# Biases of V and of the output projection as one more matmul each, x normalised on GpSimd, the residual added on VectorE, softmax divided in one pass, features later

## What is computed

```python
x = x + jnp.tanh(g_xattn[0]) * _L0_xattn_ref(_layernorm(x, axis=-1), ctx_1024, ctx_1024, ...)
x = x + jnp.tanh(g_ffn[0]) * _L0_ffn_ref(_layernorm(x, axis=-1), L0_ffn_w1, L0_ffn_w2)

# _L0_xattn_ref: 16 heads of width 32
Q, K, V = query @ Wq.T + bq, key @ Wk.T + bk, value @ Wv.T + bv
scores = Q @ K^T / sqrt(32)
feats = [scores.mean, scores.max(-1).mean, var(softmax(scores), ddof=1).mean]   # per head
t = exp(clip(w3 . gelu(w2 . gelu(w1 . feats + b1) + b2) + b3))                   # a temperature per head
out = softmax(Q @ K^T / (2 t)) @ V
return out @ Wo.T + bo

# _L0_ffn_ref: rows of x quantised to 8 bits, weights to -1, 0, 1
h = gelu(_bitlinear(x, w1)); return _bitlinear(h, w2)
```

## Time and profile before

| | |
|---|---|
| device time, median of 3 runs | 1525.43 us (1525.19 to 1525.73) |
| span of the profiled execution | 1523.1 us (the page gives no other time for it) |
| median less that span | 2.3 us |
| busy: PE, DVE, ACT, POOL | 1247.1, 1187.1, 958.2, 429.1 us |
| mean granted clock of TensorE | 0.91 |
| one turn of the loop (end of the feed-forward to the next) | 169.7 to 173.1 us |

### The profile page before, as it was taken

The page is one execution under the profiler, slowest core; times in us unless marked ns, Lnnn a source line. Parts: engine busy times, 40 slices in busy tenths (PEclk is TensorE's granted clock), DMA queues, the critical chain, the costliest instruction groups (busy, mean ns, idle before and its releaser), DMA issues.

```text
span 1523.1 us, 23233 instructions
## 1 busy us (share of the span) xinstructions
PE 1247.1 (82%) x6620; PEld 450.7 (30%) x6620; DVE 1187.1 (78%) x2082; ACT 958.2 (63%) x1559; POOL 429.1 (28%) x389
## 2 busy tenths in 40 slices
PE   3635669988898889988898889988998899778958
PEld 1201321244213332244214331244213431133224
DVE  7399769888788958888788959888688969974236
ACT  3554469755785559755785659755795658744814
POOL 5350342331325212331325213331225211210220
PEclk9855779999999999999999999999999999879979
DMA  8250130012202110012202110112202110001000
GB/s 320 63 159 0 42 86 12 30 41 50 76 2 70 43 72 15 34 37 56 70 2 70 43 72 15 37 34 52 74 2 70 43 56 1 1 0 57 1 0 28
DMA packets 34977, 73.66 MB, mean 48 GB/s; under 512 B 7456, under 2 KB 7456, under 8 KB 34336
## 3 DMA queue, kind: packets, MB, share of 16 engines
q1 hardware_dynamic: 34848, 72.10, 16.1%
HBM read 38.39 MB, written 8.39 MB: 31 GB/s over the span
## 4 chain that ended last, share of the span: by engine, by line
PE 44%; DVE 32%; issue 12%; ACT 6%; POOL 4%; DVEq 1%; DMA 1%; SPq 0%; ACTq 0%; POOLq 0%
DVE stat L827 7%; PE mm_ps L1138 6%; PE b_ps L1312 5%; DVE nmax L822 5%; PE b_ps L1163 5%; PE a_ps L1157 4%; PE b_ps L1138 4%; PE mm_ps L1178 4%; PE mm_ps L1185 3%; ACT etile L655 3%; PE o_ps L1178 3%; PE mm_ps L1291 2%; DVE hmax L952 2%; POOL xres L610 2%; PE b_ps L1291 2%
## 5 line engine op out<-in xcount | busy, mean ns | idle before, releaser
L655 ACT ACTIVATE etile<-a_ps,nmax 128x512 f32<-128x512 f32 x512 | 355.8, 697 | 251.7 <-DVE nmax L822 250.7
L822 DVE TENSOR_REDUCE nmax<-a_ps 128x1 f32<-128x512 f32 x512 | 348.8, 682 | 89.1 <-PE a_ps L1157 81.4
L665 ACT ACTIVATE region<-b_ps,inv2t 128x512 f32<-128x512 f32 x512 | 333.6, 700 | 66.9 <-PE b_ps L1163 63.3
L827 DVE BATCH_NORM_STATS2 stat<-etile 128x6 f32<-128x512 f32 x512 | 350.7, 685 | 15.5 <-ACT etile L655 13.2
L1157 PE MATMUL a_ps<-kst,qst 96*128 96x512 f16 x512 | 213.3, 418 | 105.8 <-ACT etile L655 80.7
L1163 PE MATMUL b_ps<-qst,kst 97*128 97x512 f16 x512 | 198.7, 398 | 24.1 <-ACT region L665 15.1
L583 POOL TENSOR_TENSOR region<-region 128x512 f16<-128x512 f32 x64 | 80.7, 1263 | 307.4 <-ACT region L702 307.2
L1163 PEld LDWEIGHTS b_ps<-qst,kst 97*128 97x128 f16 x512 | 49.3, 97 | 287.5 <-ACT region L665 254.4
L544 POOL TENSOR_TENSOR region<-region 128x512 f32<-128x512 f32 x32 | 40.5, 1267 | 325.2 <-DVE region L855 325.2
L569 POOL TENSOR_TENSOR xres<-xres,bo_row 128x512 f32<-128x512 f32 x32 | 39.7, 1273 | 318.0 <-DMA xres<-in_x_dram 318.0
L1157 PEld LDWEIGHTS a_ps<-kst,qst 96*128 96x128 f16 x512 | 50.6, 99 | 211.1 <-ACT etile L655 168.0
(11 more groups left out here) (218 smaller groups left out, 2038.1 us busy)
## 6 DMA issues: line engine op xcount, KB each, us to landing
kst<-region SPq DMA_DIRECT2D x96, 128.0 KB, 2.3
qst<-region SPq DMA_DIRECT2D x96, 128.0 KB, 2.3
region<-in_x_dram SPq DMA_DIRECT2D x8, 1024.0 KB, 5.4
xres<-in_x_dram SPq DMA_DIRECT2D x8, 1024.0 KB, 5.2
out_dram<-xres SPq DMA_DIRECT2D x32, 256.0 KB, 2.0
cin<-in_ctxT_dram SPq DMA_DIRECT2D x30, 256.0 KB, 5.1
kst<-in_f1T_dram SPq DMA_DIRECT2D x2, 1024.0 KB, 11.2
qst<-in_f2T_dram SPq DMA_DIRECT2D x2, 1024.0 KB, 5.4
```

The source lines that it names most:

```text
L655: nc.scalar.activation(etile[:, k % 2, :], a_ps[k % 2][:, :], ACT.Exp, bias=nmax[:, slot_of(n), t:t + 1], scale=1.0).then_inc(a_exp, 1)
L665: nc.scalar.activation(probs[:, s % 2, g, :], b_ps[g % 2][:, :], ACT.Exp, scale=inv2t[:, slot:slot + 1]).then_inc(b_exp, 1)
L822: vec.tensor_reduce(nmax[:, slot_of(k // T), k % T:k % T + 1], a_ps[k % 2][:, :], AX.X, ALU.max, negate=True).then_inc(a_max, 1)
L827: vec.bn_stats(stat[:, slot_of(k // T) * T + k % T, :], etile[:, k % 2, :]).then_inc(a_stat, 1)
```

## The change

V and W get a thirteenth matmul each, whose left side is a tile of ones and whose right side, `bias16`, holds 64 bv (or 64 bo) in row 0 as its float16 part and in row 32 as the rest. GpSimd makes `bias16` once in the setup, ahead of everything else that it does there, from two transfers that now stand next to each other. The additions of bv (L621) and bo (L569) go. VectorE adds W from PSUM to the residual (`residual`), in the place of ScalarE's copy and GpSimd's addition. GpSimd normalises x itself: a tensor_scalar in float32, a cast to float16, and the low half as before. `normalise` multiplies the output once, with a small extra instruction in its first part, and GpSimd's addition of the two parts goes. VectorE's `features` stand behind `quantise_h` of block 0, and M0 to M3 each come later in the feed-forward. Where V's readiness had a semaphore, TensorE now waits ahead of Q until all four parts of V are drained.

```diff
@@ bank_uses
-    uses += some("up0", NB, has_b) + some("up1", NB, has_b) + some("M", 2, has_a)
+    uses += some("up0", NB, has_b) + some("up1", NB, has_b)
...
-        if has_a and t < 2:
-            uses += [("M", 2 + t)]
+        if has_a and t < 3:
+            uses += [("M", 0), ("M", 1)] if t == 0 else [("M", 1 + t)]
@@ sync, setup
-            sp.dma_start(bv_row[:, :], bv.partition_broadcast(P)).then_inc(small_in, 16)
+            sp.dma_start(bias_row[:, 0, :], bv.partition_broadcast(P)).then_inc(bias_in, 16)
+            sp.dma_start(bias_row[:, 1, :], bo.partition_broadcast(P)).then_inc(bias_in, 16)
@@ gpsimd, setup
+            pool.memset(ones16[:, :], 1.0).then_inc(bias_step, 1)
+            pool.memset(bias16[:, :, :], 0.0).then_inc(bias_step, 1)
+            pool_waits.wait_ge(bias_in, 32)
+            pool.tensor_scalar(bias_hi, bias_row, WSCALE, None, ALU.mult).then_inc(bias_step, 1)
+            pool_waits.wait_ge(bias_step, 3)
+            pool.tensor_copy(bias16[0:1, :, :], bias_hi[0:1, :, :]).then_inc(bias_step, 1)
+            pool.tensor_scalar(bias_row[DK:DK + 1, :, :], bias_row[DK:DK + 1, :, :], WSCALE, None, ALU.mult) \
+                .then_inc(bias_step, 1)
+            pool_waits.wait_ge(bias_step, 5)
+            pool.tensor_tensor(bias16[DK:DK + 1, :, :], bias_row[DK:DK + 1, :, :], bias_hi[DK:DK + 1, :, :],
+                               ALU.subtract).then_inc(bias_step, 1)
+            pool_waits.wait_ge(bias_step, 6)
@@ gpsimd, split_y
-                pool.tensor_tensor(part_pos, part_pos, part_neg, ALU.add).then_inc(y_sum, 1)
-                pool_waits.wait_ge(y_sum, nth(b, C, G + 1))
@@ gpsimd, body
-                    for t in range(T):
-                        ins = pool.tensor_tensor(xres[:, t, :], xres[:, t, :], bo_row[:, :], ALU.add)
@@ gpsimd, split_x
+                    if t == 0 and has_b:
+                        pool_waits.wait_ge(y_done, nth(i - 1, C, C))
+                    pool.tensor_scalar(xin[:, t, :], xin[:, t, :], mv1[:, t, 0:1], rstd1[:, t:t + 1],
+                                       ALU.subtract, ALU.mult).then_inc(x_norm, 1)
+                    pool_waits.wait_ge(x_norm, nth(i + 1, T, t + 1))
+                    pool.tensor_copy(x_split[t][:, 0, :], xin[:, t, :]).then_inc(x_hi_done, 1)
                     pool_waits.wait_ge(x_hi_done, nth(i + 1, T, t + 1))
                     pool.tensor_tensor(x_split[t][:, 1, :], xin[:, t, :], x_split[t][:, 0, :], ALU.subtract) \
                         .then_inc(x_lo_done, 1)
...
-                        pool.tensor_tensor(xres[:, t, :], xres[:, t, :], attn[:, t, :], ALU.add).then_inc(res_done, 1)
...
-                        ins = pool.tensor_tensor(vbuf[1 - par][:, t, :], vbuf[1 - par][:, t, :], bv_row[:, :], ALU.add)
@@ scalar, body
-                        nc.scalar.activation(attn[:, t, :], mm_ps[bank_n][:, :], ACT.Copy,
-                                             scale=tg_w[:, 0:1]).then_inc(mm_free[bank_n], 1)
@@ vector, normalise
+                    c.link(vec.scalar_tensor_tensor(out=zinv[:, :], in0=z_own, scalar=0.0, in1=zwide[:, :],
+                                                    op0=ALU.is_ge, op1=ALU.mult))
...
-                    c.link(vec.scalar_tensor_tensor(out=part_pos, in0=o[:, :], scalar=0.0, in1=part_neg,
-                                                    op0=ALU.max, op1=ALU.mult))
-                    vec.scalar_tensor_tensor(out=part_neg, in0=o[:, :], scalar=0.0, in1=part_neg,
-                                             op0=ALU.min, op1=ALU.mult).then_inc(o_norm, 1)
+                    vec.scalar_tensor_tensor(out=y32, in0=o[:, :], scalar=LOWEST, in1=zrow,
+                                             op0=ALU.max, op1=ALU.mult).then_inc(o_norm, 1)
@@ vector
-            def norm_x(i, t, has_b):
+            def residual(i, t):
+                if t == 0:
+                    dve_waits.wait_ge(res_in, i * 16)
+                bank_n, before = mm_use(i, "W", t)
+                dve_waits.wait_ge(mm_full[bank_n], before + 1)
+                vec.scalar_tensor_tensor(out=xres[:, t, :], in0=mm_ps[bank_n][:, :], scalar=tg_w[:, 0:1],
+                                         in1=xres[:, t, :], op0=ALU.mult, op1=ALU.add) \
+                    .then_inc(mm_free[bank_n], 1)
@@ vector, body
-                if has_a:
-                    features(i, par)
                 if has_b:
                     scale_h(i, 0)
                     quantise_h(i, 0)
+                if has_a:
+                    features(i, par)
...
-                    if has_a and t == 1:
+                    if has_a and t == 2:
                         temperature(i)
@@ tensor, split_product
+                if bias is not None:
+                    ins = mat(mm_ps[bank_n][:, :], ones16[:, :], bias16[:, bias, :], start=False, stop=True)
@@ tensor, body, ahead of Q
                 if has_p:
                     for t in range(T):
                         drained(i, "X", t)
+                        drained(i, "V", t)
```

More of the change, by code:

```diff
@@ L602, in body @@
                     inverse_deviation(i + 1, mv1, mv1_done, var1_eps, rstd1, rstd1_done)
-                for t in range(T):
-                    if has_p and not first:
+                    pool_waits.wait_ge(rstd1_done, nth(i + 1, 1, 1))
+                    for t in range(T):
                         split_x(t)
-                    if has_b:
-                        bank_n, before = mm_use(i, "W", t)
-                        pool_waits.wait_ge(mm_free[bank_n], before + 1)
-                        pool.tensor_tensor(xres[:, t, :], xres[:, t, :], attn[:, t, :], ALU.add).then_inc(res_done, 1)
                 if has_b:
@@ L1013, in _ @@
             weight_lo(1, "v")
-            for t in range(T):
-                norm_x(-1, t, False)
             weight_lo(2, "q")
@@ L1059, in body @@
                     tiles_a(C + t)
-                    if has_p and not first:
-                        norm_x(i, t, has_b)
-                    if has_b and t > 0:
-                        residual_stat(i, t - 1)
+                    if has_b:
+                        residual(i, t)
+                        if t > 0:
+                            residual_stat(i, t - 1)
                 if has_b:
@@ L1126, in drained, with split_product @@
                 pe_waits.wait_ge(mm_free[bank_n], before + 1)
-            def split_product(bank_n, left, right, tiles=()):
+            def split_product(bank_n, left, right, tiles=(), bias=None):
                 tiles = list(tiles)
@@ L1138, in split_product @@
                     ins = mat(mm_ps[bank_n][:, :], left[l](c), right[r](c),
[L1139 removed]
+                              start=(c, l, r) == pairs[0], stop=bias is None and (c, l, r) == pairs[-1])
+                if bias is not None:
+                    ins = mat(mm_ps[bank_n][:, :], ones16[:, :], bias16[:, bias, :], start=False, stop=True)
                 ins.then_inc(mm_full[bank_n], 1)
@@ L1341, in body @@
                     if has_a and t == 0:
+                        if isinstance(i, int) and i == 0:
+                            pe_waits.wait_ge(setup_dve, SETUP_STEPS)
+                            pe_waits.wait_ge(kst_ones, 2)
+                        pe_waits.wait_ge(feat_done, nth(i, 1, 1))
+                        bank_n = take(i, "M", 0)
+                        pe_waits.stand()
+                        nc.tensor.transpose(mm_ps[bank_n][0:H * T, 0:P], nmax[:, :, :].rearrange("p h t -> p (h t)"),
+                                            ident32[:, :]).then_inc(mm_full[bank_n], 1)
+                        bank_n = take(i, "M", 1)
+                        for f in range(3):
+                            ins = mat(mm_ps[bank_n][0:DH, 0:H], w1r[:, f, :], feat[:, f, :], start=f == 0,
+                                      stop=f == 2)
+                        ins.then_inc(mm_full[bank_n], 1)
+                    if has_a and t == 1:
                         drained(i, "M", 1)
```

110 lines of the change are left out of this document (37 added, 73 removed).

## The result

The changed kernel takes 1589.3 us (median of 4 runs, 1588.1 to 1590.8) against 1525.6 before: 4.1% slower, ratio 1.041 with an interval of 1.039 to 1.043. The forecast was 1524.0, with 1540 as the upper end.

The account below looks back on a forecast made before the run. TensorE's waits for VectorE's division, GpSimd's x and block quantising were taken as the bound. Setup +5.0, turn 0 +0.5, six loop turns -8.1, turn 7 +3.0, turn 8 -1.8 gave -1.4: 1524.0 us, range 1510 to 1540.

Parts of the forecast that it names:

- the forecast's own signs of being wrong: L596 above 0.9 us, TensorE's waits in Q coming back another way, or the setup moving by more than 8.
- sets and K: Loop turn: one multiplication fewer per output group, a small instruction more; -1.1 us in the sets, -0.35 in K.
- W and x: Loop turn: x ready 11.0 us after the deviation in place of 11.8, -0.8; W's bias matmuls hidden.
- V with its biases and its wait: Loop turn: four unhidden bias matmuls on V +0.9 us; TensorE's wait for V's drain ahead of Q 0.9, net +0.7.
- feed-forward: Loop turn: features behind block 0's quantising give -0.7 us; -2.2 at full clock, 0 with a longer slow stretch.
- d: GpSimd's tensor_scalar on each part of x: taken as 0.75 us, between the cast's 0.61 and an addition's 1.26.
- the first rival: GpSimd's tensor_scalar as fast as the cast (0.61) and TensorE staying warm: 1514 us, at the far end 1509; 27%.
- costs as much as an addition (25%): Rival: GpSimd's tensor_scalar on x takes 1.26 us, so 32 parts cost +16 us, 1540; chance 25%.
- The wait inside block 2's `up`: Feed-forward: TensorE stands some 6 us until block 0's `turned_h`, then restarts at the lower clock, 1.55 us lost.
- on VectorE's way at +3.4: Turn 7: features, earlier inside a wait for gelus, now on VectorE's way, +3.4 us of the turn's +3.0 sum.
- a gain of 3.1 that did not come: Setup: bv's addition no longer contends with the ternary weights, 3.8 us, of which 3.1 count.
- Its 0.24 for a small link: Sets: the new small instruction and its link, priced like one of fourteen feature rows taking 3.5 us in turn 7.

Follow-up runs that it names:

- experiment 4: Kernel before plus 18 instructions, nine forms twice, behind the end of GpSimd's program, to price them; 1530.5 us, a single run.
- Experiment 2: Changed kernel without GpSimd's tensor_scalar that normalises x, cast and low half kept; 1511.6 us, ratio 0.9898 to the kernel before.
- Experiment 3: Changed kernel with features and the temperature's four small matmul steps back ahead of block 0's row maxima; 1559.2 us, 30.1 less than the changed kernel.
- Experiment 5: Changed kernel with x normalised on VectorE again and features ahead of block 0 again; 1514.2 us, ratio 0.9922 to the kernel before.
- Experiment 8: Kernel before with only the features and the temperature's matmul steps moved behind block 0's quantising; 1537.2 us, ratio 1.0071.
- experiment 9: Changed kernel with only TensorE's wait ahead of Q for the copy of V taken out; 1582.4 us, 6.9 less than the changed kernel.
- Experiment 1: Changed kernel with the normalising of x back on VectorE; 1542.3 us, ratio 1.0095 to the kernel before, 47 of the 64 us gone.
- Experiment 6: Kernel of experiment 5 without TensorE's wait ahead of Q for the copy of V; 1499.6 us, 14.7 less, ratio 0.9826 to the kernel before.
- Experiment 7: Kernel of experiment 6 with the four setup steps on bv and bo moved from GpSimd to VectorE; 1497.0 us, ratio 0.9809 to the kernel before.
- Experiment 10: Kernel before with only the single division: one multiplication, a small extra instruction, no GpSimd addition of output parts; 1517.4 us, ratio 0.9938.
- experiment 12: Kernel of experiment 7 with the float16 high half of x made by ScalarE in the loop; 1478.8 us, ratio 0.9676 to the kernel before.

## Why the prediction was wrong

On the profiled spans the change is +65.8 us where the sum said -1.4. Up to the first row maximum it is +17.0 (said +5.0), in turn 0 +7.6 (+0.5), in the six loop turns +40.5 (-8.1), in turn 7 +4.7 (+3.0), in turn 8 -4.1 (-1.8). Two of the forecast's own signs of being wrong came: L596 is above 0.9, and the setup moved by more than 8. By stage, as a mean of the six loop turns:

| stage | forecast, us | measured, us |
|---|---|---|
| sets and K | -1.45 | -1.46 |
| W and x | -0.8 | +5.28 |
| V with its biases and its wait | +1.6 | +2.39 |
| feed-forward | -0.7 | +0.55 |

**The step that failed: d, the length of GpSimd's tensor_scalar.** The forecast says "I take 0.75, nearer to the cast", with an addition's 1.26 as the upper bound. Measured, d is 2.07 us. The way in which d counts was right: four parts of d + 2.0 give 16.3 us behind the deviation, and 16.6 were measured. By the forecast's own slope (32 parts, each on TensorE's path) the error is 32 x 1.32 = 42 us, 5.3 in each of eight batches. The argument from the number of tensors read was wrong: with one tensor this instruction costs more than the addition of two. The rule cited beside the first rival, one-input work at roughly line rate, held in experiment 4 for copy and cast (0.61) and not for the tensor_scalar (1.50 at least). The rival "costs as much as an addition (25%)" had the direction and the mechanism, with TensorE standing before V; its size was still 0.8 us short. The forecast treated a price that no row showed as lying between two rows of other kinds, and nothing put it there. The Trainium skill (GPSIMD Engine Reference, Performance versus the Vector engine), named beside that rival, says that elementwise work belongs on VectorE. This case agrees: VectorE's tensor_scalar on the same part takes 0.54 us where GpSimd does not hold it up, and up to 1.50 beside GpSimd's work.

**The clock behind the longer wait.** The forecast had V at the speed of before. V's first part took 5.35 us in place of 3.98, of which the thirteenth matmul is 0.22 and the clock the other 1.15, behind 7.7 us of waits in place of 3.8. Experiment 2 shows the same from the other side: without the wait V runs at full clock throughout. The forecast read its rows of before too simply here: it put what exceeds 52 matmuls of 0.22 down to transposes at the lower clock, but these are 0.8 us of it, and the rest is V's own first matmuls at the lower clock.

**Feed-forward: mechanism right, size off, and the question too narrow.** The wait inside block 2's `up` came where it was forecast (`turned_h` 16.5 us behind the first `up`, said 16.3; the wait 4.96, said some 6), and so did the half speed behind it. Its cost was mis-sized: `down` 0 starts 21.8 us behind the first `up` where 21.0 was forecast, then takes 4.21 in place of 3.62, so the turn's -0.7 is +0.9 (+0.55 on average). More weighs what was not asked. The long features of before came from the addition of bv beside them, and that addition went wherever the features stand; left early they would have fitted into VectorE's wait for gelus. Experiments 3, 5 and 8 put the later place at 30, 28 and 12 us. In turn 7, where the forecast had them on VectorE's way at +3.4, experiment 3 takes 6.7 us off (159.9 to 153.2).

**Setup.** The steps on the biases end at 32.7, not 30. The two tensor_scalars take 4.55 us (beside weight instructions of VectorE) and 2.77 where the forecast had 1.0 each (its own rule, twice the cast's 0.61, gives 1.2) and up to 4.5 for such meetings; copy and subtraction, 1.23 and 2.11, are near its 1.0 and 2.2:

```profile
21.82 4.55 POOL L538 TENSOR_SCALAR vbuf<-vbuf 128x1024 f16<-128x1024 f32 x1 [8.39 <-DMA vbuf<-in_bo_dram]
26.44 1.23 POOL L540 COPY bias<-vbuf 1x1024 f16<-1x1024 f16 x1
27.75 2.77 POOL L541 TENSOR_SCALAR vbuf<-vbuf 1x1024 f32<-1x1024 f32 x1
30.61 2.11 POOL L544 TENSOR_TENSOR bias<-vbuf 1x1024 f16<-1x1024 f32 x1
...
90.03 7.95 POOL L576 MEMSET kst<- 1x8192 f16 x1 [2.26 <-DVE f L1001]
```

x is ready at 50.2 us where 41.7 was said (34.5 before), which is 8.5 of the 12.0 us that the forecast lacks in the setup; 5.3 of the 8.5 are d. The other 3.5 are in the main a gain of 3.1 that did not come: the addition of bv no longer meets the ternary weights, but the memset of 7.95 us now does, and one weight instruction of VectorE beside it took 5.64 us. No experiment took the memset away.

**What was right.** Sets and K together came as forecast, though not each for itself (-0.7 and -0.8 on average where -1.1 and -0.35 were said). Its 0.24 for a small link came from fourteen rows of which two are neighbours of the features; with twelve it is 0.29, and the forecast for both -1.2. The wait for V is 0.85 (0.9), and experiment 9 gives 6.9 us for all eight of them. Experiment 1 was expected from the changed kernel's trace with these terms, and came within 1 us.

**What stays open.** Experiments 6 and 9 take out the same wait and gain 14.7 and 6.9. Experiment 7 gains 9.6 at the first row maximum and 2.6 at the end. Experiment 10 gives in sets and K what its part should, and loses most of it again in V, and experiment 12 gains 18 where its wait and W's stage explain 7. Each time the difference stands for the most part in stages with equal work at another granted clock (turn 7: 0.89 against 0.91). Why the same instructions are granted more in one kernel than in the other was not tried. So what one edit is worth here is uncertain by up to some 10 us; the 47 and 30 us above are clear of that.

## What to carry to other kernels

A price that no row shows is not bounded by rows of other instructions: when one instruction of unknown length stands 32 times on a serial path, give that length a wide upper end, above all on an engine whose forms cost so differently (0.61, 1.26 and 2.07 us for the same 128x512). Before work is moved away from a contended place, ask whether the same change has already removed the contention. And ask which engine lies idle in the stage where x is late: ScalarE did, and half of VectorE's part of x given to it came with a gain of 18 us, 7 of them in that stage.

## What the runs showed of the hardware

GpSimd's tensor_scalar on 128x512 float32 takes 2.07 us with two operations and two pointers, and 1.50 at least (experiment 4); VectorE's takes 0.54 undisturbed.

A copy of 128x512 on GpSimd took 0.61 us in one round of experiment 4 and 1.61 in the other, a tensor_scalar with one operation 1.50 and 2.38. The longer ones lie beside VectorE's tensor_scalar of 128x2048 float32 in SBUF, 1.29 us long. GpSimd's row, and VectorE's:

```profile
1502.71 1.61 POOL L643 COPY cin<-cin 128x512 f32<-128x512 f32 x1
```

```profile
1502.57 1.29 DVE L986 TENSOR_SCALAR region<-region,hsc 128x2048 f32<-128x2048 f32 x1
```

So a VectorE instruction that reads one tensor of SBUF and writes SBUF can hold GpSimd up too, here by 0.9 to 1.0 us; VectorE's own 1.29 is its usual length. The reverse is in the kernel before: beside GpSimd's low half of x (26.15, 1.39 long) VectorE's tensor_scalar of 0.54 takes 1.38:

```profile
26.44 1.38 DVE L916 TENSOR_SCALAR region<-region,mv,rstd 128x512 f32<-128x512 f32 x1
```

The Trainium skill (SBUF — State Buffer, Who interferes with whom) says so of VectorE's modes of two ports; the rows agree in the effect and do not show the mode.
